# Row sums of causal attention: which engine sums the last two steps of query blocks 2 and 3, and where the running sum is closed

## What is computed

```
scores = einsum('bqhd,bkhd->bhqk', q, k) + einsum('bqr,bkr->bqk', q_rope, k_rope)[:, None]
scores = where(causal, -inf, scores / sqrt(HD + D_R))
w = softmax(scores, axis=-1)          # exp(s - max) / row sum of exp
attn = einsum('bhqk,bkhd->bqhd', w, v)
```

## Time and profile before

| | before |
|---|---|
| median of 3 runs | 3670.44 us (3668.8 to 3671.71) |
| the profiled execution: its own time, its span | 3666.61 us, 3664.9 us |
| busy in the span: TensorE, GpSimd, VectorE, ScalarE | 96%, 74%, 70%, 50% |
| granted TensorE clock, mean | 0.985 of full speed |
| attention stage | from about 480 to 2891 us |

### The profile page before, as it was taken

The page is one execution under the profiler, slowest core; times in us unless marked ns, Lnnn a source line. Parts: engine busy times, 40 slices in busy tenths (PEclk is TensorE's granted clock), DMA queues, the critical chain, the costliest instruction groups (busy, mean ns, idle before and its releaser), DMA issues. The chain is left out here.

```text
span 3664.9 us, 53754 instructions
## 1 busy us (share of the span) xinstructions
PE 3534.7 (96%) x19296; PEld 2402.5 (66%) x19296; DVE 2567.5 (70%) x5329; ACT 1823.1 (50%) x3455; POOL 2709.4 (74%) x1225
## 2 busy tenths in 40 slices
PE   6999969999999999999999999999999699999999
PEld 3777746666666666666666666666665488888887
DVE  5767657777777777777777777777776366666665
ACT  2334325555555555555555555555555344444443
POOL 1333328898898898988988989889898656666665
PEclk9999979999999999999999999999999899999999
DMA  5689862544634636446355353563552111111110
GB/s 179 246 285 293 284 155 68 127 97 94 143 78 109 139 76 133 91 100 137 80 113 128 87 130 84 110 136 78 116 112 77 61 58 69 69 69 70 69 69 35
DMA packets 232754, 426.54 MB, mean 116 GB/s; under 512 B 25380, under 2 KB 26916, under 8 KB 232488
## 3 DMA queue, kind: packets, MB, share of 16 engines
q1 hardware_dynamic: 232424, 423.10, 44.2%
q10 hardware_dynamic: 64, 0.02, 0.0%
HBM read 300.86 MB, written 121.65 MB: 115 GB/s over the span
## 5 line engine op out<-in xcount | busy, mean ns | idle before, releaser
L890 ACT ACTIVATE att_probs<-att_ps_s 128x512 f32<-128x512 f32 (+3 forms) x2560 | 1311.5, 535 | 978.3 <-PE att_ps_s L1048 878.8
L985 POOL TENSOR_TENSOR att_sum_g<-att_sum_g,att_probs 128x2048 f32<-128x2048 f32 (+3 forms) x432 | 1665.0, 3854 | 57.2 <-ACT att_probs L890 8.6
L925 DVE TENSOR_REDUCE att_piece_max<-att_ps_m 128x1 f32<-128x512 f32 x1536 | 970.5, 683 | 281.4 <-PE att_ps_m L1033 278.5
L1047 PE MATMUL att_ps_s<-att_q_a,att_k_a 128*128 128x512 f32 (+3 forms) x2560 | 959.9, 379 | 12.5 <-DMA att_q_b<-att_neg_max 8.8
L1048 PE MATMUL att_ps_s<-att_q_b,att_k_b 65*128 65x512 f32 (+3 forms) x2560 | 934.3, 368 | 0.0
L1033 PE MATMUL att_ps_m<-att_k_a,att_q_a 128*128 128x512 f32 (+3 forms) x1840 | 663.3, 383 | 17.4 <-PEq L215 13.7
L928 DVE CUSTOM_DVE_ANT_0 att_ps_m<-att_ps_m,mask_qk 128x128 f32<-128x128 f32 (+3 forms) x1024 | 487.1, 512 | 269.7 <-PE att_ps_m L1033 252.7
L1047 PEld LDWEIGHTS att_ps_s<-att_q_a,att_k_a 128*128 128x128 f32 x2560 | 487.4, 190 | 189.9 <-issue 87.8
L1054 PE MATMUL att_ps_o<-att_probs,att_v 128*32 128x512 f32 (+3 forms) x5120 | 552.7, 537 | 23.7 <-POOL att_probs L966 23.7
L1048 PEld LDWEIGHTS att_ps_s<-att_q_b,att_k_b 65*128 65x128 f32 x2560 | 486.2, 190 | 62.0
L1033 PEld LDWEIGHTS att_ps_m<-att_k_a,att_q_a 128*128 128x128 f32 x1840 | 348.6, 191 | 236.0 <-issue 105.0
(11 more groups left out here) (176 smaller groups left out, 4901.7 us busy)
## 6 DMA issues: line engine op xcount, KB each, us to landing
att_q_a<-s_q_hi SPq DMA_DIRECT2D x128, 256.0 KB, 6.3
att_q_a<-s_qr_hi SPq DMA_DIRECT2D x128, 256.0 KB, 7.0
prj_x_sb<-in_x_dram SPq DMA_DIRECT2D x16, 1024.0 KB, 5.3
s_q_hi<-prj_q_hi SPq DMA_DIRECT2D x16, 1024.0 KB, 4.4
s_q_lo<-prj_q_lo SPq DMA_DIRECT2D x16, 1024.0 KB, 6.5
s_k_hi<-prj_k_hi SPq DMA_DIRECT2D x16, 1024.0 KB, 4.7
s_k_lo<-prj_k_lo SPq DMA_DIRECT2D x16, 1024.0 KB, 6.9
s_v<-prj_v_sb SPq DMA_DIRECT2D x16, 1024.0 KB, 9.7
```

What stands on the lines that cost most here:

```text
L890: act.activation(probs[t % RING][:, hh, c0:CH], ps_s[(GH * t + hh) % SBANKS][:, c0:CH], ACT.Exp, scale=SCALE).then_inc(probs_ready, 1)
L925: dve.tensor_reduce(top, ps_m[:, bank, :], AX_X, ALU.max).then_inc(piece_taken, 1)
L985: pool.tensor_tensor(sum_g[:, :, c0:CH], sum_g[:, :, c0:CH], new, ALU.add).then_inc(sum_added, 1)
L1047: mm(out[:, c0:CH], k_a[:, hh, i * P:(i + 1) * P], q_a[j][:, hh, c0:CH], start=True, stop=False)
```

## The change

Four things change in the attention stage.

- `SHARE_OF` of blocks 2 and 3: the last two steps (256 and 128 queries wide) go from G to T, the first diagonal step (512 wide) from T to G. Block 3 keeps its T at step 6.
- For blocks that end with T (0, 2 and 3) the closing comes ahead of the products of the last two steps, and VectorE waits for those products (`pv_done`) instead of the closing.
- In block 2 the closing now opens `ps_d`; in block 3 step 6 opens it as before.
- GpSimd's order in blocks 2 and 3: the additions of steps 4j-1 and 4j stand behind the clearing of step 4j+1.

```
-SHARE_OF = ("GGTT", "GGGGGGGG", "GGGGGGGGTGGG", "GGGGGGTGGGGGTGGG")
+SHARE_OF = ("GGTT", "GGGGGGGG", "GGGGGGGGGGTT", "GGGGGGTGGGGGGGTT")
+ENDS_ON_PE = [owners[-1] == "T" for owners in SHARE_OF]
+OPENED_BY_SUM = ["T" not in owners.rstrip("T") for owners in SHARE_OF]
...
-            if j == 0:
+            if ENDS_ON_PE[j]:
                 return pv_done, NSTEP * u + FIRST[j] + STEPS[j] + RING
             return closed, TCH * u + j + 2
...
-                    if j == 2:
-                        order.remove(("add", TB * j - 1))
-                        order.insert(order.index(("clear", TB * j + 1)) + 1, ("add", TB * j - 1))
+                    if j >= 2:
+                        for i in (TB * j, TB * j - 1):
+                            order.remove(("add", i))
+                            order.insert(order.index(("clear", TB * j + 1)) + 1, ("add", i))
...
-                    first = j > 0 and i == SHARE_OF[j].index("T")
+                    first = not OPENED_BY_SUM[j] and i == SHARE_OF[j].index("T")
...
-                    last = over_keys(ps_d, ones, probs[s % RING], start=first, stop=(j == 0 and i == STEPS[j] - 1), c0=c0)
+                    last = over_keys(ps_d, ones, probs[s % RING], start=first, stop=(i == STEPS[j] - 1), c0=c0)
...
-                opens = j == 0 or "T" not in SHARE_OF[j]
+                opens = OPENED_BY_SUM[j]
...
-                last = over_keys(ps_d, ones, sum_g, start=opens, stop=(j > 0))
+                last = over_keys(ps_d, ones, sum_g, start=opens, stop=not ENDS_ON_PE[j])
...
-                if closing and closing[1] == 0:
+                if closing and ENDS_ON_PE[closing[1]]:
                     parts.append(lambda: close_denominators(*closing))
...
-                if closing and closing[1] > 0:
+                if closing and not ENDS_ON_PE[closing[1]]:
```

## The result

| | before | after |
|---|---|---|
| median of 4 runs | 3670.06 us (3668.8 to 3671.71) | 3727.47 us (3727.0 to 3731.13) |
| profiled execution: its own time, its span | 3666.61 us, 3664.9 us | 3727.0 us, 3725.3 us |
| TensorE, GpSimd busy | 96%, 74% | 95%, 74% |
| mean granted clock | 0.985 | 0.976 |

The change makes the kernel slower: ratio 1.0159, 95% interval 1.0145 to 1.0174. Forecast were 3720 us in a range of 3688 to 3742.

What follows compares the result with a forecast made beforehand. GpSimd was taken to bound each unit from block 0's closing to block 2's, TensorE the rest. 3666.6 + 25.4 (15 units, full clock) + 2 (last unit) + 24.9 (clock) = 3718.9, forecast 3720 us, range 3688 to 3742.

Steps and rivals of the forecast that it cites:

- Two stretches, GpSimd's up to block 2's closing and TensorE's behind it: Per unit, GpSimd sets the time from block 0's closing to block 2's, TensorE the next 73.09 us.
- GpSimd's 1057.06 for step 9's sum and the closing 0.25 us earlier: Block 2, unit 3: GpSimd's additions end at 1057.06, closing starts at about 1057.15 instead of 1057.40.
- A stand of 1.3 and 2.3 us: End of block 2: TensorE idles 1.3 us at the fourth head's score and 2.3 us ahead of the closing.
- the ring: Block 3's second-step exponentials wait for step 8's addition until 1053.56, delaying the fourth head's score (about 0.6 us).
- +1.60 us for the products out of the shadow: Behind block 2's closing: last two steps' products, sums and two maxima pieces delay the scores, 1.60 us a unit.
- -0.21 for the sums: Block 3: TensorE loses step 12's sum (0.86) and gains those of 14 and 15 (0.65), net -0.21 us.
- +0.3 us for block 3's wait: Block 3's closing: TensorE waits 0.3 us for additions held behind the clearing of step 13; bounds 0 and 2 us.
- Rival 2: GpSimd late in block 3 too: wait 2 us instead of 0.3, 3744 us; chance 0.10.
- The clock falls in most units, at 2.0 us each: Behind block 2's closing TensorE's clock drops after the longer stand: 30 us less 5.1 already paid, +24.9 us.
- Rival 1: The clock holds after block 2's stands, leaving only the full-clock costs: 3694 us; chance 0.17.
- The last unit, +2 us: Last unit's end is GpSimd's: 1.05 us more adding, plus four products between closing and reciprocals, +2 us.
- Rival 3: Faster: GpSimd finishes step 9 before TensorE arrives at block 2's closing, gaining 2.4 us a unit, 3626 us; chance 0.08.

Runs made afterwards that it cites:

- e8_order_filler: Changed kernel with block 3's step 11 added ahead of the clearing of steps 12 and 13, and eight extra matmuls before block 2's closing: 3684.4 us, ratio 1.0047.
- e7: Kernel before with only block 2's closing moved ahead of the products of the last two steps: 3702.5 us, ratio 1.0096.
- e11: Kernel before with block 2's closing moved ahead of the last two steps' products and ten extra matmuls in the stand before it: 3683.0 us, ratio 1.0044.
- e4_filler: Changed kernel with eight extra matmuls, results overwritten, in the stand ahead of block 2's closing: 3700.0 us, ratio 1.0083.
- e5_three_t: Kernel before with block 2's last two steps also on TensorE, step 8 kept there, closing in front; block 3 unchanged: 3640.9 us, ratio 0.9930.
- e3: Changed kernel with block 3's addition of step 11 moved back ahead of the clearing of steps 12 and 13: 3708.9 us, ratio 1.0107.
- e6: Kernel before with block 2's new shares only, closing behind the products, steps 10 and 11 cleared right behind step 7's addition: 3687.7 us, ratio 1.0054.
- e1_block2: Changed kernel with block 3 put back as before, so only block 2 is changed: 3709.0 us, ratio 1.0107.

## Why the prediction was right

- *Two stretches, GpSimd's up to block 2's closing and TensorE's behind it.* Held. From block 2's closing to block 0's lie 73.09 us before and 1297.29 - 1220.05 = 77.24 after, 4.15 us more; this part took the whole loss of the unit. GpSimd's part, from block 0's closing to block 2's, is 73.7 us in the median unit where it was 74.05.
- *GpSimd's 1057.06 for step 9's sum and the closing 0.25 us earlier.* Held: 0.21 (42.51 us after the block's first addition, 42.72 before). Not foreseen was that block 1's closing comes 0.17 us earlier as well, where nothing had been changed; why is not shown.
- *A stand of 1.3 and 2.3 us, the first one through the ring.* Measured 1.29 and 2.11.
- *+1.60 us for the products out of the shadow, -0.21 for the sums.* The sum of both is 1.15 us a unit by e8_order_filler, a sixth less than the 1.39. Counted from the closings, the prediction has 1.60 + 0.25 - 0.21 = 1.64 us behind block 2's closing, and e8_order_filler shows 1.6; what is missing is the 0.45 us that GpSimd's stretch gave back instead of 0.25. e7 and e11 show an effect of the same kind with none of the shares moved, which is the strongest evidence that it is the position and not the work.
- *+0.3 us for block 3's wait.* Right mechanism, wrong size: 1.04 us, and 1.1 of the period. TensorE's arrival was the mis-sized term. GpSimd was through 13.7 us after step 13's exponentials (13.6 predicted, with a tenth or two for the signal); TensorE was there 12.7 us after them, and not 13.4; why it came earlier was not found. Rival 2 had this wait at 2 us; the truth lay between it and the forecast. This term is 11 us too low over 15 units and the one above 4 us too high, and together they are the 7 us by which the forecast was low: the total came out closer than its largest miss.
- *The clock falls in most units, at 2.0 us each.* It fell in all 15 behind the first, at 2.0 us each by e4_filler: about 1.6 for the short ones and 2.8 for the longer ones, nine to five, which is close to the weighting that the prediction had chosen from two short cases and a long one. With three cases to go by, that it hit the average so well is partly luck. Rival 1, the clock that holds, is refuted by the windows. By the rule of "TensorE: Matmul & The Clock Gate", section "Why this matters for your kernels", in the Trainium skill it would have held, since each idle gap (1.29 and 2.11 us) is shorter than those which the section warns of; the measurement decides against that here.
- *The last unit, +2 us.* 104.7 us from block 2's first addition to the last reciprocals, 103.3 before: 1.4.
- *Rival 3, faster.* The point that it named, step 9's sum 3.7 us earlier, is what e5_three_t creates by leaving one full addition (4.7 us) out. The gain was then 1.4 us a unit and the falls of the clock, not rival 3's 2.4. The difference is work that e5 keeps on TensorE: with step 8's sum (0.86) in block 2 and without block 3's saving (0.21), rival 3's sum gives 1.3.

The size in all: 25.4 us at full clock predicted against 2.2 x 15 = 33 measured, 24.9 for the clock against 2.05 x 15 - 4.6 = 26 (4.6 being what the two falls before the change had cost), and 2 against 1.4 for the last unit.

## What to carry to other kernels

Where two engines take turns as the bound, ask of each moved piece of work what it stood beside: TensorE work beside a wait for GpSimd was free, and the same work behind that wait cost its full time (1.6 us a unit in e8_order_filler, of 1.64 counted); an edit that moved nothing but a position lost 35 us. When a wait must be shortened, take work from the engine that is waited for and pay for it elsewhere (e5) rather than swap shares of equal size, and never put an operation whose data is there behind one whose data is not (e3). A stand can cost more through the clock behind it (1.5 to 2.0 us a unit here) than the moved work costs at full clock (1.15 and 1.25), so count stands close together as one, and price what follows them at the lower clock too.

## What the runs showed of the hardware that had not been expected

- TensorE's granted clock fell after stands of 1.3 and 2.1 us with 0.85 us of matmuls between them in every one of 15 units, after a single one of 3.0 us in 13 of 15 (e7), and after 1.1 and 0.4 us in 2 of 14 (the kernel before). In e6 it fell in 9 of the 12 units with a stand of 2.1 us or more, and in none of the three with 0.6 to 1.1 us. In the first unit, after a stand of 1.9 us, it held in the change and fell in e1_block2 and e3_order. So the same stand is followed by a fall in some units and executions and not in others. Eight idle-time matmuls, 1.9 us of work whose result nobody reads, kept it up in nearly all units and made the kernel 27.5 us faster.
- At 1.2 GHz a closing took 1.86 us instead of 1.00, and a fall cost 2.0 us a unit on average: 1.5 to 1.6 for most, about 2.8 for those in which the clock stayed low about twice as long.
- One kernel falls a different number of times from execution to execution: the kernel before ran between 3664.2 and 3678.8 us, at a mean granted clock of 0.985 and 0.981 of full speed. The missing 0.004 of some 3670 us would be 15 us (an estimate from these two figures), which is the size of the difference.
